# q's product ahead of the transpositions, its whole chain in one group, and the values' wait split by pairs

## What is computed

```
xn = layernorm(x) * g_norm
q  = xn @ Wq            -> 16 heads of 64, each row divided by its norm, times q_scale
kv = xn @ Wkv           -> one k and one v; a null key and value are put in front
sim  = 8 * q k^T + bias(relative position)    (causal)
attn = softmax(sim);  out = (attn @ v) @ Wout;  y = layernorm(out) * g_out
xq = fake_quant(y);  h = silu(xq @ Wgate^T) * (xq @ Wup^T)
result = x + fake_quant(h) @ Wdown^T
```

## Time and profile before

| | us |
|---|---|
| median of 3 runs (299.69 to 299.98) | 299.69 |
| the profiled execution | 299.08 |
| its span, first to last instruction | 297.3 |
| TensorE busy, matmuls (share of the span) | 257.9 (87%) |
| VectorE busy | 238.1 (80%) |
| ScalarE busy | 230.0 (77%) |
| GpSimd busy | 204.6 (69%) |

### The profile page before, as it was taken

One profiled execution on the slowest core, in us unless ns is written; L12 is line 12 of the kernel. 1 busy time (PEld: TensorE's weight loads), 2 busy tenths in 40 slices (PEclk: granted clock), 3 DMA queues, 4 the chain that ended last, 5 costly groups with the idle time before them and its releaser, 6 DMA issues.

```text
span 297.3 us, 7308 instructions
## 1 busy us (share of the span) xinstructions
PE 257.9 (87%) x2161; PEld 203.5 (68%) x2162; DVE 238.1 (80%) x969; ACT 230.0 (77%) x781; POOL 204.6 (69%) x394
## 2 busy tenths in 40 slices
PE   0769999999999999999999999999999989975270
PEld 0427777787888778877887888788878767751060
DVE  2768978798879878888888798787877788869893
ACT  1554978888898899889988988889888897259380
POOL 2277979788878887887888888788877785013300
PEclk9989999999999999999999999999999999999857
DMA  4179100000000000000000000000000020000013
GB/s 142 33 191 264 21 1 2 1 2 1 3 0 2 4 1 2 0 3 1 2 0 4 3 0 2 0 4 0 2 0 4 1 73 3 2 0 0 1 37 110
DMA packets 13084, 6.89 MB, mean 23 GB/s; under 512 B 1954, under 2 KB 12914, under 8 KB 13043
## 3 DMA queue, kind: packets, MB, share of 16 engines
q1 hardware_dynamic: 11874, 6.03, 7.7%
q10 hardware_dynamic: 1168, 0.36, 0.6%
HBM read 5.31 MB, written 1.07 MB: 21 GB/s over the span
## 4 chain that ended last, share of the span: by engine, by line
PE 60%; DVE 20%; POOL 8%; issue 5%; DMA 4%; ACT 2%; SPq 1%; POOLq 0%; DVEq 0%; ACTq 0%
PE bank L904 14%; PE front L881 7%; PE bank L855 7%; PE back L947 7%; PE bank L744 6%; POOL prob L448 6%; PE back L881 5%; PE front L947 4%; DVE score L1276 4%; DMA g1b<-in_L_cond_g_dram 4%; PE bank L760 3%; DVE oT L1266 2%; DVE hmax L1428 2%; DVE oT L1464 2%; DVE yn L1299 1%
## 5 line engine op out<-in xcount | busy, mean ns | idle before, releaser
L589 ACT ACTIVATE prob<-score,negmax 128x258 f32<-128x258 f32 (+1 forms) x256 | 113.4, 449 | 17.8 <-DVE negmax L1276 17.7
L448 POOL TENSOR_SCALAR prob<-prob,rrow 128x258 f32<-128x258 f32 x254 | 107.9, 443 | 22.0 <-DVE rrow L1284 20.1
L401 POOL TENSOR_TENSOR rq<-qn,neghalf 128x8 f32<-128x8 f32 x32 | 53.3, 1666 | 2.7
L589 ACT ACTIVATION_READ_ACCUMULATOR prob<-score,negmax 128x1 f32 x256 | 49.2, 192 | 0.0
L904 PE MATMUL bank<-pT,val 128*64 128x256 f32 x496 | 47.1, 332 | 0.0
L1276 DVE CUSTOM_DVE_ANT_0 score<-front,bias 128x258 f32<-128x258 f32 (+1 forms) x128 | 38.2, 354 | 8.0 <-PE front L881 7.8
L904 PEld LDWEIGHTS bank<-pT,val 128*64 128x64 f32 x496 | 30.8, 136 | 19.3 <-ACT pT L599 9.9
L1145 DVE TENSOR_REDUCE qn<-sq 128x8 f32<-128x512 f32 x32 | 21.9, 684 | 23.7 <-ACT sq L535 23.7
L1276 DVE CUSTOM_DVE_ANT_0 score<-back,bias 128x258 f32<-128x258 f32 (+1 forms) x128 | 38.0, 353 | 0.1
L855 PE MATMUL bank<-wout,oT 128*128 128x128 f32 x256 | 36.7, 287 | 1.2 <-DVE yn L1299 1.1
L599 ACT COPY pT<-back 128x384 f32<-128x384 f32 x62 | 28.8, 481 | 9.0 <-PE back L947 8.6
(11 more groups left out here) (203 smaller groups left out, 465.0 us busy)
## 6 DMA issues: line engine op xcount, KB each, us to landing
bias<-relative_table SPq DMA_DIRECT2D x8, 256.0 KB, 5.0
out_dram<-prob SPq DMA_DIRECT2D x4, 256.0 KB, 3.0
X<-in_x_dram SPq DMA_DIRECT2D x1, 896.0 KB, 13.9
prob<-in_L_cond_Wq_dram SPq DMA_DIRECT2D x1, 512.0 KB, 5.4
wout<-in_L_cond_Wout_dram SPq DMA_DIRECT2D x1, 512.0 KB, 15.1
prob<-in_L_ffn_w_down_dram SPq DMA_DIRECT2D x1, 176.0 KB, 2.4
X<-in_x_dram SPq DMA_DIRECT2D x1, 128.0 KB, 4.3
prob<-in_L_ffn_w_gate_dram SPq DMA_DIRECT2D x1, 128.0 KB, 2.2
```

Source lines behind the costliest of these rows:

```text
L401: pool.tensor_tensor(dst, src, neghalf[:, 0:width], ALU.pow).then_inc(done, 1)
L448: pool.tensor_scalar(prob[:, par, h, cols], prob[:, par, h, cols], rrow[:, par, h, t:t + 1], 1.0, ALU.mult, ALU.mult).then_inc(normed, 1)
L589: act.activation(prob[:, par, h, cols], score[:, h % 4, cols], ACT.Exp, scale=-1.0, bias=negmax[:, par, h, t:t + 1], accum_out=rowsum[:, p ...
```

## The change

TensorE makes q's product between the products with Wout (and `y_null`) and the turns. All of q's preparation for that quarter follows in the same group: ScalarE squares it after the group's first two exponents, VectorE sums it after inverting the sums of heads 0 and 1, GpSimd takes its power after normalising the late heads of the group before and ahead of the early heads of this one. q's normalisation stands first in the next group on VectorE. The powers of x, y and k move beside it, y's into g = 1 and k's into g = 0; y's statistics move ahead of q's sums, y's normalisation ahead of the copy of `oT`. In the first batch the low part of x is made before the scores of group 1. The values wait for two heads' `pT` before each pair, where they waited for all four at once.

```diff
--- before.py
+++ after.py
@@ -449,18 +449,18 @@
                                            1.0, ALU.mult, ALU.mult).then_inc(normed, 1)
 
             def group(s):
-                if s.kT is not None:
-                    k_power(s.kT)
-                if s.g == 2 and s.prev is not None:
-                    y_power(s.prev)
-                if s.g == 3 and s.b + 3 < B:
-                    x_power(s.b + 3)
-                if s.quarter is not None and s.quarter >= 4:
-                    q_power(s.quarter, s.quarter % 4)
                 if s.turned is not None:
                     normalise(heads(s.turned)[2:4])
                 if s.at == 2:
                     x_power(2)
+                if s.g == 3 and s.b + 3 < B:
+                    x_power(s.b + 3)
+                if s.g == 1 and s.prev is not None:
+                    y_power(s.prev)
+                if s.made is not None:
+                    q_power(s.made, s.made % 4)
+                if s.kv is not None:
+                    k_power(s.kv)
                 normalise(heads(s.at)[0:2])
                 if s.b == B - 1 and s.g == 1:
                     pool.wait_ge(n_done, s.b)
@@ -469,7 +469,6 @@
 
             def ending():
 
-                y_power(B - 2)
                 normalise(heads(LOOP - 1)[2:4])
                 for at in (LOOP, LOOP + 1):
                     normalise(heads(at)[0:2])
@@ -609,8 +608,6 @@
                    .then_inc(w_a, 1)
 
             def group(s):
-                if s.quarter is not None and s.quarter >= 4:
-                    q_square(s.quarter, q_ps)
                 if s.turned is not None:
                     exponent(heads(s.turned)[2])
                     exponent(heads(s.turned)[3])
@@ -620,6 +617,8 @@
                 if s.at == 0:
                     xT_evac(1, halves(misc))
                 exponent(heads(s.at)[1])
+                if s.made is not None:
+                    q_square(s.made, q_ps)
                 if s.turned is not None:
                     pT_evac(s.turned, 0)
                     pT_evac(s.turned, 1)
@@ -887,10 +886,6 @@
             def values(at):
 
                 m, g = at // GB, at % GB
-                if at == LOOP:
-                    pe.wait_ge(pTe_ready, GH)
-                else:
-                    pe.wait_ge(pT_ready, GH * (at if at > LOOP else at + 1))
                 if g == 0:
                     pe.wait_ge(v_ready, m + 1)
                 last_group = at == GB * B - 1
@@ -899,6 +894,10 @@
                 if at > 0 and not last_group:
                     pe.wait_ge(oT_ready, at)
                 for pair in range(2):
+                    if at == LOOP:
+                        pe.wait_ge(pTe_ready, 2 * pair + 2)
+                    else:
+                        pe.wait_ge(pT_ready, GH * (at - 1 if at > LOOP else at) + 2 * pair + 2)
                     for blk, c0, c1, i0 in ((1, 0, N, 0), (0, N, N + P, P)):
                         for a in range(2):
                             last = pe.matmul(ps[a * D:a * D + D, pair * N + i0:pair * N + N], val[m % 2][:, blk, :],
@@ -1029,6 +1028,12 @@
                     y_products(s.summed, 1)
                 if s.g == 1 and s.prev is not None:
                     y_null(s.prev)
+                if s.made is not None:
+                    if s.made % 4 == 0:
+                        if s.first:
+                            pe.wait_ge(wq_low, 1)
+                        pe.wait_ge(xT_low, s.next)
+                    q_make(s.made, s.made % 4, s.made // 4 % 2, q_ps)
                 if s.turned is not None:
                     turn(s, 0)
                     turn(s, 1)
@@ -1037,12 +1042,7 @@
                 if s.turned is not None:
                     turn(s, 2)
                     turn(s, 3)
-                if s.made is not None:
-                    if s.made % 4 == 0:
-                        if s.first:
-                            pe.wait_ge(wq_low, 1)
-                        pe.wait_ge(xT_low, s.next)
-                    q_make(s.made, s.made % 4, s.made // 4 % 2, q_ps)
+
             def over_partitions(k):
 
                 pe.wait_ge(f_v, 1 + 3 * k)
@@ -1321,12 +1321,15 @@
                                       None, ALU.mult).then_inc(last_normed, 1)
 
             def group(s):
-                if s.quarter >= 4:
-                    q_norm2(s.quarter, s.quarter % 4)
-                if s.summed is not None:
-                    oT_copy(s.summed)
                 if s.g == 2 and s.prev is not None:
                     y_normalise(s.prev)
+                    oT_copy(s.summed)
+                if s.quarter >= 4:
+                    q_normalise(s.quarter, s.quarter % 4, q_ps)
+                if s.summed is not None and not (s.g == 2 and s.prev is not None):
+                    oT_copy(s.summed)
+                if s.at == 1:
+                    xT_split_low(1, 1)
                 if s.first:
                     dve.wait_ge(ld_bias[s.g], 16 * 2)
                 score_pair(heads(s.at)[0:2])
@@ -1334,17 +1337,18 @@
                     invert(heads(s.turned)[2:4])
                 if s.kT is not None:
                     k_normalise(s.kT)
-                if s.quarter >= 4:
-                    q_normalise(s.quarter, s.quarter % 4, q_ps)
                 score_pair(heads(s.at)[2:4])
                 if s.at == 0:
                     qT_evac(2, 2, 0)
                     q_normalise(3, 3, q_ps0[3])
                 invert(heads(s.at)[0:2])
+                if s.g == 1 and s.prev is not None:
+                    y_stats(s.prev)
+                if s.made is not None:
+                    q_norm2(s.made, s.made % 4)
                 if s.quarter > 2:
                     qT_evac(s.quarter, s.quarter % 4, s.quarter // 4 % 2)
                 if s.at == 1:
-                    xT_split_low(1, 1)
                     x_stats(2)
                 if s.at == 2:
                     x_normalise(2)
@@ -1354,8 +1358,6 @@
                     k_norm2(s.kv)
                 if s.g == 0 and s.prev is not None and s.b + 2 < B:
                     x_normalise(s.b + 2)
-                if s.g == 1 and s.prev is not None:
-                    y_stats(s.prev)
                 if s.g == 2 and s.b > 1:
                     yT_absmax(s.b - 2)
                 if s.g == 3 and s.prev is not None and s.b + 2 < B:
@@ -1373,8 +1375,8 @@
                 score_pair(heads(LOOP)[0:2])
                 invert(heads(LOOP - 1)[2:4])
                 score_pair(heads(LOOP)[2:4])
+                y_normalise(B - 2)
                 oT_copy(LOOP - 2)
-                y_normalise(B - 2)
                 invert(heads(LOOP)[0:2])
                 ffn_weights(0)
                 score_pair(heads(LOOP + 1)[0:2])
```

## The result

The changed kernel takes 302.68 us (median of 4 runs, 301.68 to 303.47) against 299.69 for the kernel before (299.12 to 299.98): a ratio of 1.0109, with a 95% interval of 1.0071 to 1.0146. It is slower by 3.0 us, where 1.3 were predicted (301.0). A second set of runs gave 301.80 against 298.91, 1.0105 [1.0061, 1.0149]. The profiled execution took 302.30, its span is 300.4.

What follows compares the result with a forecast made beforehand. The prediction took q's chain, not TensorE, as the bound after the change. 2.2 - 1.2 - 0.1 + 0.1 + 0.3 = +1.3 us on 299.69 gave 301.0; own range 299.0 to 302.9, stated range 296.5 to 303.8.

Steps and rivals of the forecast that it cites:

- the steady state: From group 4's scores over six batches: batches 1 to 4 take 29.25 each, 5 and 6 28.70; 2.2 us longer.
- the first batch: Start of the kernel: q's product no longer waits for xTl and group 2 starts earlier; gain 1.2, bounds 0.5 and 1.9.
- the end: Last batch: y's power delays the weights' padding by 1.5, so the last scores come later; loss 0.3, bounds 0 and 1.5.
- The ring: q's chain through ScalarE, GpSimd and VectorE, from a group's scores (s) to the next group's: 7.00 a group, setting the pace.
- Rival 1: TensorE stays the bound and the ring is shorter than read: 28.4 a batch, 296.8 us; chance 0.25.
- the fourth step: Fourth group of batches 1 to 4: x's small power ahead of q's on GpSimd lengthens it to 7.55.
- the second group: Second group of a batch: y's statistics and power stand ahead of q's; the third group's scores start 7.70 later.
- The keys' power stands behind q's and ahead of the early normalisations ...: nothing: On GpSimd: the early normalisations are needed by the next group's turns only some 2 us later, so no cost charged.
- group 2 starts 0.9 to 1.0 earlier: First batch: wait of 0.54 and product's 0.87 gone, some 0.5 given back; group 2's scores earlier than 40.81.
- plain steps: Groups with nothing in between in q's chain: 7.00 from one group's scores to the next's.
- TensorE alone: TensorE's own pace after the move: 28.7 less 0.8 of gaps plus 0.44 of new stall, 28.3 to 28.4 a batch.
- Rival 2: x's normalisation on VectorE is blocked until q's power on GpSimd ends: +3.0, 304.0 us; chance 0.13.

Runs made afterwards that it cites:

- e4_ofirst: The changed kernel with oT's copy put ahead of q's normalisation on VectorE in every group: 294.48 us, ratio 0.9861.
- e7_kone: The changed kernel with the keys' normalisation reading one operand from SBUF instead of two, leaving out the product with qks: 299.86 us, ratio 1.0043.
- e3_mult: The changed kernel with q's power on GpSimd replaced by a multiplication from the second batch's q on: 291.11 us, ratio 0.971.
- e6_both: The changed kernel with oT's copy ahead of q's normalisation and x's small power behind q's in the fourth group: 293.49 us, ratio 0.9798.

## Why the prediction was right or wrong

301.0 was forecast and 302.68 measured, inside the stated range of 296.5 to 303.8. The direction and what sets the pace were right; two terms were too favourable, the steady state by 1.5 us and the first batch by 0.9 (of which 0.33 is a later start), and the end takes 0.5 back. The forecast's own range of 2 us either way holds for eight errors of 0.03 that are independent of one another; if they all went one way over 24 groups it would be 5.8.

**Right: what sets the pace.** The ring worked out from the earlier trace rows came to 7.00 and measures 6.95; its points are within 0.04 (sums at s + 2.84 for 2.88, GpSimd 3.73 for 3.76, q's normalisation 5.75 for 5.78), and the copy of oT is 0.60 for the estimated 0.61. The wait of VectorE for `rq` in all groups, 1.3 us a batch of idle TensorE, and the fourth step of 7.54 (7.55) came as told. Rival 1, that the copy comes ahead of the power's end, fell with VectorE's written order, and e4_ofirst shows what the copy ahead would have given (294.48). Scores of group 4 were to be at about 55.0; they are at 55.83.

**Wrong by size: the second group, 8.02 for 7.70.** The failed step is "The keys' power stands behind q's and ahead of the early normalisations ...: nothing". It looked at who waits for those, and not at what runs beside them. Timeline of before, VectorE and GpSimd, at the same place:

```profile
121.86 0.58 DVE L1134 SCALAR_TENSOR_TENSOR kz<-kv,rk,qks 128x128 f32<-128x128 f32 x2
...
122.15 1.82 POOL L448 TENSOR_SCALAR prob<-prob,rrow 128x258 f32<-128x258 f32 x4 [0.45 <-DVE rrow L1284]
```

There kz (the keys' normalisation) started in a gap of GpSimd. After, the keys' power holds the early normalisations back until 121.57, they close up with the late ones to a block of eight until 124.91, and kz starts in its middle, at 122.92: 0.94 instead of 0.58, and everything behind it on VectorE is 0.36 later. y's statistics stand at s + 3.27 for the s + 2.91 worked out, q's normalisation at s + 7.41, the scores at s + 8.02: the whole of the 0.32 that was missing. e7_kone takes 0.36 from this step and none from another, 2.2 us from group 4 to 28 (175.85 to 173.66), so this pair of kz does set the step. That the keys' power is what brings the block beside it is read from these rows; no run moves that power.

The steady state was missed by 1.45 (3.69 for 2.2): six second groups 0.32 too short are 1.92, batch 5's step of 7.21 for 7.00 adds 0.21, and thirteen plain steps of 6.95 for 7.00, with the fourth steps' 0.01, give 0.69 back.

**Wrong by size: the first batch, 0.34 in the span for 1.2.** Counted from the first scores, which came 0.33 later (they lie anywhere from 27.6 to 29.7 in the profiles of the kernels here, so this is not the change's), the gain is 0.67. The failed step is "group 2 starts 0.9 to 1.0 earlier": from the first scores to those of group 2 it is 11.81 for 12.42, a gain of 0.61. (The 1.2 was also rounded up, as its own terms come to 1.1.) TensorE takes 3.48 from the product's start at 34.01 to the scores of group 2, where turns, idle time and product took 4.09 (33.68 to 37.77). The idle 0.54 is gone, but the product's 0.87 isn't: it still stands ahead of these scores, now before the turns. What it gave by moving is that the turns run closer, less a new wait. Timeline of the changed kernel:

```profile
35.91 0.60 PE L759 MATMUL bank<-ident,qn 128*128 128x128 f32 x4
...
36.55 0.69 DVE L1156 COPY qT<-bank 128x512 f32<-128x512 f32 x1
...
37.49 0.93 PE L880 MATMUL front<-kT,qT 64*128 64x258 f32 x8 [0.33 <-ACT pT L598]
...
40.53 0.42 DVE L1276 CUSTOM_DVE_ANT_0 score<-front,bias 128x258 f32<-128x258 f32 x1
```

The scores of group 2 need the last quarter of qT. TensorE's transpositions of it stand behind the product and end at 36.51, and VectorE's copy runs to 37.24; the turns of heads 2 and 3 end at 37.17, and TensorE is idle for 0.33. The row names ScalarE's copy of pT, but the kernel asks there for the first two copies of group 1 alone, which were done by 36.59. Before, the product stood between the turns and the scores and covered this wait, as it covered the values'. This is read from the rows and the kernel's waits; no run tests it. Groups 2 and 3 took 15.30 (15.2 worked out).

**Wrong and of no weight: TensorE alone.** 28.3 to 28.4 were worked out, 27.81 is what e3_mult shows. The gaps that the move closes were put at 0.8 at most, from the 0.41 of recorded idle time, and are 1.0 a batch; the new stall was put at 0.11 a group and is 0.04 (from the start of the values to the scores 1.49 in three groups of four of e3_mult, and 1.45 in the second, which has none, as in all of the kernel before). The move is thus worth 0.9 us a batch and not 0.3, if nothing else is bound. It changes nothing for the kernel as it was written, whose ring is longer, and is why e6_both can be 2% faster than before.

**Right: x's normalisation isn't blocked.** Rival 2 had it held until q's power ends. The two take 0.60 from 119.23, beside a power from 118.81 to 120.48, as in the earlier trace rows. The charge of nothing stands. What the prediction didn't see is that in the kernel before the same two take 0.89 (at 117.71), beside GpSimd's normalisations: the move made them shorter, in a place where VectorE then waits for the power anyway (0.68 at 120.51).

**The end.** The wait for the weights came as foreseen. Timeline, VectorE:

```profile
249.64 0.95 DVE L1237 TENSOR_REDUCE wmax<-prob 128x6 f32<-128x768 f32 x1 [2.10 <-DMA prob<-in_L_ffn_w_down_dram]
250.51 0.42 DVE L1276 CUSTOM_DVE_ANT_0 score<-front,bias 128x258 f32<-128x258 f32 x1
```

The last scores stand right behind it, where the earlier trace rows has 1.11 between. The last two steps are 0.06 and 0.10 longer (5.07 for 5.01, 6.80 for 6.70): 0.16 for the 0.4 reckoned. The first of the batch gains 0.16 (6.95 for 7.11) for 0.1. Net nothing, for +0.3. The 0.2 that the rest gained after the last scores was not followed.

## What to carry to other kernels

When a step is moved into the group that it belongs to, follow it once round every in-order queue that it passes, from one iteration's start to the next's: the sum of the hops is a pace of its own, and an engine that was busy for 28.29 of 28.70 us is no longer the bound if that sum is larger. What stands in the ring behind the step without needing it (here one 0.6 us copy) costs its full length each time, and belongs into the wait ahead of it. And of an instruction that is only postponed, look not only at who waits for it but at what will now run beside it.

## What the runs showed that was not expected

- Who pays when VectorE and GpSimd work on memory side by side: kz, which starts inside GpSimd's block, 450 ns in the median for 332, the block nothing (3.34 for eight). Where kz starts first, as in before at 121.86, it keeps its 0.58 and GpSimd's four take 1.82 for the usual 1.66. Where q's power starts with xTl or 0.01 after it, xTl keeps its 0.41 and the power takes 1.92 to 1.93 for 1.67. In all three the one that started first kept its length, but that is no rule: in e4_ofirst kz starts at 120.50, 0.36 after a GpSimd normalisation, and keeps 0.59, while GpSimd's four from 119.79 take 1.93; in e7_kone a power that starts at 17.98, ahead of three kz, takes 1.78. None of this was tested by itself.
- What is paid is less than the other's length: 0.26 for the power beside 0.41 of xTl, 0.36 for two kz with GpSimd's normalisations beside them from end to end.
- Which GpSimd instruction stands beside counts: x's two normalisations, each 128x128 with one tensor operand, take 0.89 beside GpSimd's normalisations (117.71 in the kernel before) and 0.60 beside its power.
- The idle time recorded on TensorE understates what can be had: 0.41 a batch in the record, 1.0 by the gain in e3_mult. That modelled ends of matmuls count as busy is the likely reason; it was not tested.
